# Attention values with the value matrix stationary in column groups, turned back in place

## The chip, the core and the metric

One core of one Trainium2 chip. The metric is the device time of one launch, in microseconds. One launch computes 32 batches of 128 tokens of 512 features. The kernel before takes 2767.58 us, the median of 3 runs (2760.34 to 2768.54).

## What is computed

```python
# attention: 32 heads of 16 features; own keys/values from x, adapter keys/values from ctx
q, k, v = (split_heads(layernorm(x) @ W) for W in (Wq, Wk, Wv));  q, k = rope(q), rope(k)
w = softmax(q @ k.T / 4 + mask)                      # own path
a_k, a_v = split_heads(ctx @ Wk), split_heads(ctx @ Wv)
a_w = tanh(gate) * softmax(q @ a_k.T / 4)            # adapter path, a gate per head
x = x + (w @ v + a_w @ a_v) @ Wo
# experts: 8, the 2 best of each token, rows sorted by expert
x = x + moe(layernorm(x), router_w, w1, w2)
```

## The kernel before

The program has two stages. `attention_phase` goes over the 32 batches and ends with the lists of tokens for each expert; `expert_phase` runs 71 tiles of tokens through their experts. The change lies in the first.

In the attention stage each engine has its own instruction stream, and its `step(b, c, d, n, m)` is run once for each batch b. One step works on several batches at once: the values of batch b; on n = b+1 the projections, rotation, scores and maxima; on d = b-1 the output chain; on c = b-2 the entering into the expert lists; on m = b+2 the first norm. Batches 4 to 29 are a loop of two steps, the others are written out. Between engines stand semaphores: an `Event` is counted up by the producer, and a `wait_ge` in the consumer's stream holds that and everything behind it. The streams are strictly in the order in which they are written, so the order of calls in `step` is the schedule.

On TensorE a step is a loop over 16 units u, a unit being four heads of one of two paths (own and adapter). Each runs `scores_T(b, u)` (transposed scores into a bank `st`), then whatever is hung at that u, then `values(b, u-1)`. ScalarE's loop over u takes the exponent `exps(b, u)` (L528) of `st` into `pr`, an fp32 tile of keys by queries for 4 heads, and does the hung copies and fp16 splits. Hung at TensorE's units before: q after unit 1; k, `ctx_turn` and `out_turn` at 2; `places` (the router's counts, which need `sel` of DVE's `router_top`) at 3; `out_project` at 4; `ak` (keys of ctx, needing ScalarE's `ctx_turned`) at 5; `h_turn` at 7, `router` at 8; `stack(n, g)` and `scores(n, g)` from 8 on, g = 0 to 7, one a unit. `stack` 0 needs DVE's `ak_low`. Behind the loop: v, avp, `x_turn`, `max_turn` (the split maxima are transposed), whose result DVE copies to `mT` (L731). The first `scores_T` of the next step waits for it.

`values` (L1097), for each head: `pr[:, path, j, :]` (128 keys by 128 queries, fp32) is the stationary operand, and the head's 17 columns of `vv` (16 features and a column of ones, whose product is the sum of the exponents) are streamed. The result is 128 queries by 17 columns of a bank `av`; a bank holds 8 heads by 2 paths, and there are two banks, used in turn. Each fp32 matmul is two passes of weight load and matmul in the trace.

DVE copies each full bank to `avs` in SBUF (`values_out`, L737). The next step begins with `norm_out` (L742 reciprocal of the sums, L744 times the gate, L746 adapter half times it), GpSimd's `own_out` (L411, the own half) and `sum_out` (L757) into `nat`. Then the output chain goes on: `out_hi` (ScalarE L538) and `out_low` (DVE L761) split into fp16, `out_turn`, `out_T`, `out_project`, `residual` (L767), norm (GpSimd L416, DVE L781), `h_high`, `h_low` (L786), `ak_low` (L676, of batch n), `h_turn`, `router`.

DVE's `rotate_q` (L685, L689) reads the projected q; GpSimd adds (L376), ScalarE writes `q_high` (L501), GpSimd the rest (L379, `qs`); only then may `rotate_k` write the same `t1`, `t2`, and the same follows for k with `k_high` (L506). ScalarE's `ctx_turned` is L480. GpSimd's `w_slice` (L402, L405) splits the expert weights. GpSimd's `enter_lists` issues 8 indirect DMAs a batch.

## Time and profile before

| what | value |
| --- | --- |
| median of 3 runs | 2767.58 us |
| the profiled execution | 2786.29 us |
| its span, first to last instruction | 2784.5 us |
| mean granted TensorE clock | 0.83 |
| TensorE matmul, busy | 2405.2 us (86%) |
| TensorE weight load, busy | 1746.0 us (63%) |
| VectorE (DVE) | 1409.8 us (51%) |
| ScalarE (ACT) | 1178.9 us (42%) |
| GpSimd (POOL) | 946.0 us (34%) |
| costliest group: values matmuls, L1097 | 636.5 us, 4096 of 292 ns |
| their weight loads | 628.6 us, 4096 of 233 ns |

The profile is of one execution, by the hardware profiler. PE is TensorE's matmuls, PEld its weight loads. Busy time is the union of the instructions of a group; matmuls are pipelined, so the mean duration of one is longer than the distance between two. The clock is given as a share of 2.4 GHz, 0.50 being 1.2 GHz. In the views in order of time, neighbouring instructions of one line stand in one row, and brackets give the idle time before it and the engine that ended it. "Low" and "high" below are the fp16 splits unless the clock is meant.

### The profile page before, as it was taken

What the parts mean: (1) busy time and instruction counts of PE and PEld (TensorE: products, weight loads), DVE (VectorE), ACT (ScalarE), POOL (GpSimd) and SP (SyncE); (2) the same over time, 40 slices, a digit from 0 to 9 for tenths busy, and PEclk for the clock granted to TensorE, in tenths of its full rate; (3) what the DMA queues carried; (4) which work ended last, traced back from release to release, by engine and by line L of the source; (5) the groups of instructions that cost most, each with busy time, mean ns of one, the idle gap of its engine ahead of it and who ended that gap; (6) DMA issues with size and microseconds to landing.
All of it is one profiled execution on the core that took longest, in us unless ns stands there. A gap on an engine that the chain in (4) does not pass through costs nothing. (4 is left out here: it accounts for less than half of the span.)

```text
span 2784.5 us, 55409 instructions
## 1 busy us (share of the span) xinstructions
PE 2405.2 (86%) x18441; PEld 1746.0 (63%) x18442; DVE 1409.8 (51%) x4993; ACT 1178.9 (42%) x2100; POOL 946.0 (34%) x948
## 2 busy tenths in 40 slices
PE   4999898889888979898888888888888836999997
PEld 2777666667666756576666666666666624666664
DVE  4466555556555645555555555555555433333332
ACT  3554444444444434344444444444444304444443
POOL 2223333333333333333333333333333223444443
PEclk7898887788788878787878787888788858999999
DMA  2010000000000000010000000000000204444444
GB/s 88 15 38 28 22 23 23 22 23 22 23 22 23 22 13 27 11 32 17 27 16 27 18 25 21 22 23 22 23 22 19 44 14 106 83 83 83 83 83 68
DMA packets 65264, 98.06 MB, mean 35 GB/s; under 512 B 24512, under 2 KB 28608, under 8 KB 64512
## 3 DMA queue, kind: packets, MB, share of 16 engines
q0 software_dynamic: 24096, 37.51, 7.7%
q1 hardware_dynamic: 40928, 57.30, 6.8%
q8 instruction: 156, 2.56, 0.4%
q14 instruction: 84, 0.69, 0.1%
HBM read 59.12 MB, written 35.65 MB: 34 GB/s over the span
## 5 line engine op out<-in xcount | busy, mean ns | idle before, releaser
L1097 PE MATMUL av<-vv,pr 128*128 128x17 f32 x4096 | 636.5, 292 | 6.2 <-ACT pr L528 6.2
L1097 PEld LDWEIGHTS av<-vv,pr 128*128 128x128 f32 x4096 | 628.6, 233 | 20.2 <-ACT pr L528 6.8
L528 ACT ACTIVATE pr<-st 128x512 f32<-128x512 f32 x512 | 305.0, 596 | 587.0 <-PE st L1083 408.6
L707 DVE TENSOR_REDUCE mx<-md 128x4 f32<-128x512 f32 x256 | 176.7, 690 | 340.4 <-remote 214.4
L1051 PE MATMUL md<-kk,qz 128*128 128x128 f16 x2048 | 214.9, 255 | 136.1 <-DVE mx L707 74.7
L1415 PE MATMUL y<-w1s,hgT 128*128 x1704 | 279.2, 314 | 4.4 <-ACT hgT L1329 4.4
L425 POOL DMA_INDIRECT lists<-row,posi x256 | 249.6, 975 | 85.4 <-issue 85.4
L710 DVE CUSTOM_DVE_ANT_0 md<-md,msk 128x128 f32<-128x128 f32 x1024 | 265.0, 321 | 0.0
L1051 PEld LDWEIGHTS md<-kk,qz 128*128 128x128 f16 x2048 | 157.4, 115 | 167.8 <-issue 112.3
L411 POOL TENSOR_TENSOR avs<-avs,rc 128x512 f32<-128x512 f32 x32 | 34.6, 1082 | 662.8 <-DVE rc L742 662.8
L1074 PE MATMUL st<-qz,kk 128*128 128x256 f16 x1024 | 213.8, 293 | 27.8 <-issue 20.1
L520 ACT ACTIVATE qz<-ma 64x256 f16<-64x256 f16 x512 | 191.6, 374 | 104.4 <-remote 86.7
L1083 PE MATMUL st<-mT,hsel 96*128 96x128 bf16 x2048 | 225.7, 238 | 1.1 <-issue 1.1
L1415 PEld LDWEIGHTS y<-w1s,hgT 128*128 128x128 f16 x1704 | 164.2, 98 | 95.8 <-issue 4.9
L737 DVE COPY avs<-av 128x272 f32<-128x272 f32 x128 | 56.5, 441 | 313.9 <-PE av L1097 278.0
L1083 PEld LDWEIGHTS st<-mT,hsel 96*128 96x128 bf16 x2048 | 153.3, 107 | 94.9 <-issue 84.7
L1078 PE MATMUL st<-identr,mskp 128*128 128x512 f32 x512 | 209.5, 495 | 0.0
L522 ACT ACTIVATE kk<-ma 128x512 f16<-128x512 f16 x256 | 152.9, 597 | 3.0
L1434 PE MATMUL y<-w2s,yT 128*128 (+1 forms) x639 | 150.3, 379 | 0.9 <-DVE yT L1393 0.9
L982 PE MATMUL ma<-w_v,xT 128*128 128x512 f16 x384 | 146.5, 559 | 0.0
L710 DVE DVE_READ_ACCUMULATOR2_ANT mx<- 128x1 f32 x1024 | 145.0, 142 | 0.0
L1329 ACT ACTIVATE hgT<-px 128x1024 f16<-128x1024 f16 x71 | 72.7, 1024 | 156.7 <-PE px L1405 156.7
(200 smaller groups left out, 3968.7 us busy)
## 6 DMA issues: line engine op xcount, KB each, us to landing
wst<-in_w SPq DMA_DIRECT2D x32, 352.0 KB, 3.3
cin<-in_ctx SPq DMA_DIRECT2D x32, 256.0 KB, 3.5
xin<-in_x SPq DMA_DIRECT2D x32, 256.0 KB, 3.7
out<-x SPq DMA_DIRECT2D x32, 256.0 KB, 2.0
h_pairs<-ohs SPq DMA_DIRECT2D x32, 256.0 KB
lists<-row,posi POOLq DMA_INDIRECT x256
msk<-in_mask SPq DMA_DIRECT2D x32, 64.0 KB, 3.1
lrow<-lists SPq DMA_DIRECT2D x71, 1.0 KB, 3.6
```

The source lines that it names most:

```text
L425: pool.indirect_dma_start(out=dram["lists"], out_offset=bass.IndirectOffsetOnAxis(ap=posi[:, e:e + 1], axis=0), in_=row[:, e, :], in_offse ...
L520: act.activation(qz[r, pairs, j, :], bank[r, 0:2], ACT.Copy)
L522: act.activation(kk[:, :, pairs, :], keys, ACT.Copy).then_inc(stk_o.sem, 1)
L528: act.activation(pr[:, path, :, :], st[path][:, :, :], ACT.Exp).then_inc(p_ex.sem, 1)
L707: dve.tensor_reduce(mx[:, 1, 4 * g:4 * g + 4], sm[1][:, :, :], AX.X, ALU.max).then_inc(s_ad.sem, 1)
L710: i = dve.tensor_tensor_reduce(sm[0][:, j, :], sm[0][:, j, :], msk[:, n.par, :], 1.0, -3.4028235e38, ALU.add, ALU.max, mx[:, 0, h:h + 1])
L1051: i = pe.matmul(sm[path][:, j, :], qz[:, h // 2, h % 2, :], keys[:, h // 2, :], start=True, stop=True)
L1074: pe.matmul(bank[:, 2 * j:2 * j + 2, :], keys[:, p, :], qz[:, p, :, :], start=(j == 0), stop=False, skip_group_check=True)
L1078: pe.matmul(bank[:, :, :], mskp[:, n.par, part, :], identr[:, :].unsqueeze(1).to_broadcast([P, 4, P]), start=False, stop=False, skip_group ...
L1083: i = pe.matmul(bank[:, j, :], hsel[:, h:h + 1].to_broadcast([3 * NH, P]), mT[:, path, :], start=False, stop=(j == 3), skip_group_check=True)
L1097: i = pe.matmul(av[g // 2 % 2][:, h % 8, path, :], pr[:, path, j, :], vv[:, n.par, path, h, :], start=True, stop=True)
L1415: i = pe.matmul(y1[s.par][j][:, 0:F], hgT[:, s.par, a, c, :], w, start=(n == 0), stop=(n == 11))
```

## The change

Four things.

1. `values` takes the 17 columns of `vv` as the stationary operand and streams the 128 queries of `pr`. Head j of a unit writes 17 partitions from partition 32j, so the four heads lie in four column groups of the array. A bank is now [128, 4, 128]: partitions are heads by columns, the rest queries.
2. The result is the wrong way round. ScalarE copies each full bank to `avT` in SBUF (`values_T`), TensorE turns it back by four fp32 transposes into the same bank (`values_back`).
3. DVE normalizes each bank straight from PSUM (`normal`: reciprocal, gate, product, sum into the new tile `on`), four times a batch, three of them among the maxima and one between the split of the maxima and the copy of `mT`. `values_out`, `norm_out`, `sum_out` and GpSimd's `own_out` are gone. The bank is free for new values when its sum is written.
4. The order of the output chain and of what lies around it is another in the streams of ScalarE, DVE and TensorE.

The diff, without declarations of events and the first and last batch:

```diff
--- before.py
+++ after.py
@@ -141,8 +142,10 @@
...
     pr = sb("pr", [P, 2, 4, P], F32)
-    avs = sb("avs", [P, NH, 2, VW], F32)
-    rc = sb("rc", [P, NH, 2], F32)
+    avT = sb("avT", [P, 4, P], F32)
+    rc = sb("rc", [P, 2, 8], F32)
+    part2 = sb("part2", [P, 2, 8, HD], F32)
+    on = sb("on", [P, D], F32)
     nat = sb("nat", [P, D], F32)
...
@@ -169,7 +172,7 @@
     st = [ps(f"st{k}", [P, 4, P], F32) for k in range(2)]
-    av = [ps(f"av{k}", [P, 8, 2, VW], F32) for k in range(2)]
+    av = [ps(f"av{k}", [P, 4, P], F32) for k in range(2)]
     ma = [ps(f"ma{k}", [P, 512], F32) for k in range(2)]
...
@@ -379,8 +383,6 @@
...
         def step(b, c, d, n, m):
-            if d:
-                own_out(d)
             w_slice(b)
...
@@ -405,12 +407,6 @@
...
-        def own_out(n):
-            pool.wait_ge(n_rc.sem, n_rc.at(n))
-            pool.tensor_tensor(avs[:, :, 0, 0:HD], avs[:, :, 0, 0:HD],
-                               rc[:, :, 0:1].to_broadcast([P, NH, HD]), ALU.mult).then_inc(n_o1.sem, 1)
         def norm_h(n):
...
@@ -527,6 +522,12 @@
...
+        def values_T(n, o):
+            act.wait_ge(av_pe.sem, av_pe.at(n, 4 * o + 4))
+            act.wait_ge(v_back.sem, v_back.at(n, o))
+            act.activation(avT[:, :, :], av[o % 2][:, :, :], ACT.Copy).then_inc(v_T.sem, 1)
         def w_slice(n):
...
@@ -535,7 +536,7 @@
...
             act.wait_ge(h2_st.sem(n.shift(-1)), h2_st.at(n.shift(-1)))
-            act.activation(ohs[:, 0, :], nat[:, :], ACT.Copy).then_inc(o_hi.sem, 1)
+            act.activation(ohs[:, 0, :], on[:, :], ACT.Copy).then_inc(o_hi.sem, 1)
...
@@ -561,32 +562,34 @@
...
                 if u == 0:
+                    if d:
+                        out_hi(d)
                     if n:
...
                     w_slice(b)
-                if u == 1 and d:
-                    out_hi(d)
                 if u == 2 and n:
                     q_high(n)
-                if u == 2 and c:
+                if u == 3 and c:
                     router_exp(c)
                 if u == 3 and n:
+                    k_high(n)
                     ctx_turned(n)
-                if u == 3 and d:
+                if u == 4 and d:
                     out_T(d)
-                if u == 4 and n:
-                    k_high(n)
-                if u == 5 and d:
-                    h_high(d)
+                if u >= 5 and u % 4 == 1:
+                    values_T(b, u // 4 - 1)
                 if u == 6 and n:
...
                 if u == 7 and d:
+                    h_high(d)
+                if u == 8 and d:
                     h_transposed(d)
...
                     stack_out(n, u - 8)
+            values_T(b, 3)
             if n:
...
@@ -652,6 +655,8 @@
...
         dve.wait_ge(pool_c.sem, pool_c_all)
+        for bank in av:
+            dve.memset(bank[:, :, :], 0.0)
         dve.tensor_copy(ident16[:, :], identf[:, :]).then_inc(dve_c.sem, 1)
...
@@ -727,38 +732,31 @@
...
             dve.tensor_copy(p3[2], mr[:, :, :]).then_inc(mp3.sem, 1)
+            if b:
+                normal(b, 3)
             dve.wait_ge(mp_t.sem, mp_t.at(n))
...
-        def values_out(n, o):
-            dve.wait_ge(av_pe.sem, av_pe.at(n, 4 * o + 4))
+        def normal(n, o):
+            bank = av[o % 2][:, :, :].rearrange("p (a g) (j c) -> p a (g j) c", a=2, c=VC)
+            dve.wait_ge(v_back.sem, v_back.at(n, o + 1))
+            dve.reciprocal(rc[:, :, :], bank[:, :, :, HD]).then_inc(n_rc.sem, 1)
+            dve.wait_ge(n_rc.sem, n_rc.at(n, o + 1))
+            dve.tensor_tensor(rc[:, 1, :], rc[:, 1, :], tg[:, 8 * o:8 * o + 8], ALU.mult).then_inc(n_rg.sem, 1)
+            dve.wait_ge(n_rg.sem, n_rg.at(n, o + 1))
+            dve.tensor_tensor(part2[:, :, :, :], bank[:, :, :, 0:HD],
+                              rc[:, :, :].unsqueeze(3).to_broadcast([P, 2, 8, HD]), ALU.mult).then_inc(n_o2.sem, 1)
+            dve.wait_ge(n_o2.sem, n_o2.at(n, o + 1))
             if o == 0:
-                dve.wait_ge(n_o.sem, n_o.at(n.shift(-1)))
-            dve.tensor_copy(avs[:, 8 * o:8 * o + 8, :, :], av[o % 2][:, :, :, :]).then_inc(av_s.sem, 1)
-        def norm_out(n):
-            dve.wait_ge(av_s.sem, av_s.at(n))
-            dve.reciprocal(rc[:, :, :], avs[:, :, :, HD]).then_inc(n_rc.sem, 1)
-            dve.wait_ge(n_rc.sem, n_rc.at(n))
-            dve.tensor_tensor(rc[:, :, 1], rc[:, :, 1], tg[:, :], ALU.mult).then_inc(n_rg.sem, 1)
-            dve.wait_ge(n_rg.sem, n_rg.at(n))
-            dve.tensor_tensor(avs[:, :, 1, 0:HD], avs[:, :, 1, 0:HD],
-                              rc[:, :, 1:2].to_broadcast([P, NH, HD]), ALU.mult).then_inc(n_o2.sem, 1)
-        def sum_out(n, x_batch):
-            if x_batch:
-                dve.wait_ge(x_hi.sem, x_hi.at(x_batch))
-                dve.wait_ge(x_lo.sem, x_lo.at(x_batch))
-            dve.wait_ge(n_o1.sem, n_o1.at(n))
-            dve.wait_ge(n_o2.sem, n_o2.at(n))
-            dve.wait_ge(h_hi.sem, h_hi.at(n.shift(-1)))
-            dve.wait_ge(h_lo.sem, h_lo.at(n.shift(-1)))
-            dve.tensor_tensor(heads(nat), avs[:, :, 0, 0:HD], avs[:, :, 1, 0:HD], ALU.add).then_inc(n_o.sem, 1)
+                dve.wait_ge(o_hi.sem, o_hi.at(n.shift(-1)))
+                dve.wait_ge(o_lo.sem, o_lo.at(n.shift(-1)))
+            dve.tensor_tensor(heads(on)[:, 8 * o:8 * o + 8, :], part2[:, 0, :, :], part2[:, 1, :, :],
+                              ALU.add).then_inc(n_o.sem, 1)
...
             dve.wait_ge(o_hi.sem, o_hi.at(n))
-            dve.tensor_tensor(ohs[:, 1, :], nat[:, :], ohs[:, 0, :], ALU.subtract).then_inc(o_lo.sem, 1)
+            dve.tensor_tensor(ohs[:, 1, :], on[:, :], ohs[:, 0, :], ALU.subtract).then_inc(o_lo.sem, 1)
...
@@ -774,10 +772,11 @@
...
-        def norm_h(n):
+        def norm_h(n, x_batch):
             dve.wait_ge(h_rs.sem, h_rs.at(n))
-            dve.wait_ge(o_hi.sem, o_hi.at(n))
-            dve.wait_ge(o_lo.sem, o_lo.at(n))
+            if x_batch:
+                dve.wait_ge(x_hi.sem, x_hi.at(x_batch))
+                dve.wait_ge(x_lo.sem, x_lo.at(x_batch))
             dve.tensor_scalar(nat[:, :], x2[:, :], mv[:, 1, 0:1], mv[:, 1, 3:4], ALU.subtract,
...
@@ -853,31 +852,27 @@
...
         def step(b, c, d, n, m):
-            if d:
-                norm_out(d)
-                sum_out(d, n)
             if n:
                 ctx_lo(n)
-                mask_lo(n)
             if d:
...
             if n:
-                rotate_q(n)
+                mask_lo(n)
             if c:
                 router_top(c)
-                router_counts(c)
             if n:
+                rotate_q(n)
                 rotate_k(n)
             if c:
+                router_counts(c)
                 router_weights(c)
-            values_out(b, 0)
             if d:
                 residual(d)
-                norm_h(d)
+                norm_h(d, n)
                 h_low(d)
...
                 ak_low(n)
-            values_out(b, 1)
+            normal(b, 0)
             if d:
...
@@ -888,15 +883,17 @@
...
                 maxima(n, 1)
-                maxima(n, 2)
-            values_out(b, 2)
+            normal(b, 1)
             if n:
-                for g in range(3, 7):
+                for g in range(2, 5):
                     maxima(n, g)
-            values_out(b, 3)
+            normal(b, 2)
             if n:
-                maxima(n, 7)
-                neg_max(n)
+                for g in range(5, 8):
+                    maxima(n, g)
+                neg_max(n, b)
+            else:
+                normal(b, 3)
...
@@ -1091,12 +1086,19 @@
...
             if u % 4 == 0:
-                pe.wait_ge(av_s.sem, av_s.at(n, u // 4 - 1))
+                pe.wait_ge(n_o.sem, n_o.at(n, u // 4 - 1))
             for j in range(4):
                 h = 4 * g + j
-                i = pe.matmul(av[g // 2 % 2][:, h % 8, path, :], pr[:, path, j, :], vv[:, n.par, path, h, :],
-                              start=True, stop=True)
+                i = pe.matmul(av[u // 4 % 2][VC * j:VC * j + VW, 2 * path + g % 2, :], vv[:, n.par, path, h, :],
+                              pr[:, path, j, :], start=True, stop=True)
             i.then_inc(av_pe.sem, 1)
+        def values_back(n, o):
+            pe.wait_ge(v_T.sem, v_T.at(n, o + 1))
+            for k in range(4):
+                i = pe.transpose(av[o % 2][:, k, :], avT[:, k, :], identf[:, :])
+            i.then_inc(v_back.sem, 1)
...
@@ -1131,21 +1133,24 @@
...
                     k(n)
+                if u == 3 and d:
+                    out_turn(d)
+                if u == 3 and n:
                     ctx_turn(n)
-                if u == 2 and d:
-                    out_turn(d)
-                if u == 3 and c:
+                if u == 4 and c:
                     places(c)
-                if u == 4 and d:
-                    out_project(d)
                 if u == 5 and n:
                     ak(n)
-                if u == 7 and d:
+                if u == 5 and d:
+                    out_project(d)
+                if u >= 6 and u % 4 == 2:
+                    values_back(b, u // 4 - 1)
+                if u == 8 and d:
                     h_turn(d)
-                if u == 8 and d:
-                    router(d)
                 if u >= 8 and n:
                     stack(n, u - 8)
+                if u == 9 and d:
+                    router(d)
                 if u >= 9 and n:
...
@@ -1155,6 +1160,7 @@
...
                 avp(n)
+            values_back(b, 3)
             if m:
...
             if n:
```

## Rows read from the trace of the kernel before

**Rows 1.** Line 731: count, duration in ns, first and last start.
```profile
L731 DVE COPY mT<-md x32: 286/287/290, 70.9 to 2193.1; 96x256 bf16<-96x256 bf16 x32
```

**Rows 2.** Slices: length, busy time by engine, granted clock, DMA share, GB/s.
```profile
1941.00:1943.00 2.00, 2.00 (x12) 1.23 (x11) 0.00 (x0) 0.00 (x0) 1.40 (x1) 0.88 0.00 0
...
1965.00:1967.00 2.00, 1.67 (x11) 1.67 (x11) 0.28 (x3) 0.35 (x1) 1.69 (x2) 0.60 0.03 1
...
1985.00:1987.00 2.00, 2.00 (x9) 0.85 (x8) 0.00 (x0) 0.53 (x1) 0.00 (x0) 0.78 0.00 0
```

**Rows 3.** TensorE in order of time, first half: start, duration, line, names, count.
```profile
1921.58 0.39 PE L1074 MATMUL st<-qz,kk 128*128 128x256 f16 x2 [0.38 <-DVE mT L731]
...
1934.91 0.19 PE L1124 MATMUL md<-sel,tri 128*128 128x8 bf16 x1 [2.68 <-DVE sel L818]
...
1938.41 4.28 PE L982 MATMUL md<-w_o,oT 128*128 128x512 f16 x12
...
1943.78 2.75 PE L982 MATMUL ma<-w_k,cT 128*128 128x512 f16 x12
1946.37 0.96 PE L1097 MATMUL av<-vv,pr 128*128 128x17 f32 x8
...
1951.93 0.27 PE L1027 MATMUL ma<-ident,qs 128*128 128x128 f16 x2
```

**Rows 4.** TensorE in order of time, second half of that batch.
```profile
1952.26 1.02 PE L1097 MATMUL av<-vv,pr 128*128 128x17 f32 x8
1953.13 0.38 PE L1074 MATMUL st<-qz,kk 128*128 128x256 f16 x2
...
1965.73 1.84 PE L1097 MATMUL av<-vv,pr 128*128 128x17 f32 x8
1967.40 0.59 PE L1074 MATMUL st<-qz,kk 128*128 128x256 f16 x2
...
1981.54 4.90 PE L982 MATMUL ma<-w_v,xT 128*128 128x512 f16 x12
```

**Rows 5.** DVE in order of time, same batch, first half.
```profile
1921.23 0.29 DVE L731 COPY mT<-md 96x256 bf16<-96x256 bf16 x1 [5.05 <-PE md L1058]
...
1928.12 0.68 DVE L685 TENSOR_TENSOR t<-ma,rope 128x512 f32<-128x512 f32 x1
...
1931.60 0.23 DVE L802 TENSOR_SCALAR key<-lg,top 128x8 f32<-128x8 f32 x1
...
1932.07 2.12 DVE L808 SCALAR_TENSOR_TENSOR key<-oh,key 128x8 f32<-128x8 f32 x1
...
1935.47 0.69 DVE L685 TENSOR_TENSOR t<-ma,rope 128x512 f32<-128x512 f32 x1
...
1943.88 0.68 DVE L767 SCALAR_TENSOR_TENSOR x<-md,xres 128x512 f32<-128x512 f32 x1
...
1948.35 0.69 DVE L786 TENSOR_TENSOR ohs<-nat,ohs 128x512 f16<-128x512 f32 x1 [0.70 <-ACT ohs L549]
1949.84 1.29 DVE L676 SCALAR_TENSOR_TENSOR aks<-ma,aks 128x512 f16<-128x512 f32 x2 [0.80 <-ACT aks L486]
```

**Rows 6.** GpSimd in order of time, same batch.
```profile
1922.06 1.08 POOL L411 TENSOR_TENSOR avs<-avs,rc 128x512 f32<-128x512 f32 x1 [19.50 <-DVE rc L742]
...
1932.04 2.13 POOL L379 TENSOR_TENSOR qs<-t,qs 128x1024 f16<-128x1024 f32 x1 [1.17 <-ACT qs L501]
```

**Rows 7.** ScalarE in order of time, same batch.
```profile
1932.76 1.02 ACT L480 ACTIVATE cT<-ma 128x1024 f16<-128x1024 f16 x1
...
1939.15 1.05 ACT L506 ACTIVATE ks<-t 128x1024 f16<-128x1024 f32 x1
```

**Rows 8.** Groups of ScalarE and DVE by line: busy us, mean ns.
```profile
L528 ACT ACTIVATE pr<-st 128x512 f32<-128x512 f32 x512 | 305.0, 596 | 587.0 <-PE st L1083 408.6 <-remote 171.5 <-PE av L1097 5.8
...
L689 DVE TENSOR_TENSOR t<-ma,rope 128x256 f32<-128x256 f32 x128 | 47.5, 411 | 0.0
...
L742 DVE RECIPROCAL rc<-avs 128x64 f32<-128x64 f32 x32 | 17.5, 546 | 33.0 <-issue 32.9
```

More of the change, by code:

```diff
@@ L39 @@
 VW = HD + 1
+VC = 32
 LB = 4
@@ L202, in attention_phase @@
     m_part, mp3, mp_t, m_T = ev("m_part", 4), ev("mp3"), ev("mp_t"), ev("m_T")
-    t_pe, p_ex, av_pe, av_s = ev("t_pe", 2 * GROUPS), ev("p_ex", 2 * GROUPS), ev("av_pe", 2 * GROUPS), ev("av_s", 4)
-    n_rc, n_rg, n_o1, n_o2, n_o = (ev(n) for n in ("n_rc", "n_rg", "n_o1", "n_o2", "n_o"))
+    t_pe, p_ex, av_pe, n_o = ev("t_pe", 2 * GROUPS), ev("p_ex", 2 * GROUPS), ev("av_pe", 2 * GROUPS), ev("n_o", 4)
+    v_T, v_back = ev("v_T", 4), ev("v_back", 4)
+    n_rc, n_rg, n_o2 = (ev(n, 4) for n in ("n_rc", "n_rg", "n_o2"))
     o_hi, o_lo, o_tp, o_T, o_p, x_2 = (ev(n) for n in ("o_hi", "o_lo", "o_tp", "o_T", "o_p", "x_2"))
@@ L439, in last @@
             pool.iota(iot, pattern=[[1, SLOTS]], base=0, channel_multiplier=0).then_inc(iot_d.sem, 1)
-            own_out(n)
             norm_h(n)
@@ L712, in maxima, with neg_max @@
             i.then_inc(s_own.sem, 1)
-        def neg_max(n):
+        def neg_max(n, b=None):
             dve.wait_ge(s_own.sem, s_own.at(n))
@@ L912, in last @@
         def last(n):
-            norm_out(n)
-            sum_out(n, None)
             router_top(n.shift(-1))
@@ L919, in last @@
             residual(n)
-            norm_h(n)
+            norm_h(n, None)
             h_low(n)
```

## The prediction

> **What bounds the kernel now.** I read the page first (time shares), then the stretch of the attention loop in one batch, engine by engine, in order of time, and last the granted clock in slices of that batch. The copy of the transposed maxima, line 731, comes once a batch and marks its end: 32 times from 70.9 to 2193.1 us, so 2122.2/31 = 68.46 us a batch [rows 1]. I take the batch from 1921.23 us on [rows 5] as the type and count its times from there ("+6.9"). TensorE carries the batch, with a few short stalls. The reader should see three things. First, the values matmuls (line 1097) are led by their weight loads: a unit of four heads is 8 loads of a 128-column fp32 `pr` and 8 matmuls of 17 columns, and the next work starts 0.87 us after it at full clock (1952.26 to 1953.13) and 1.67 us after it at 1.2 GHz (1965.73 to 1967.40) [rows 4]; 16 units make 14 us at full clock, 20% of a batch. Second, TensorE's stalls cost twice. It waits 2.68 us for the router's choice before `places` [rows 3], and runs at 1.2 GHz behind it: 12 matmuls of `out_project` take 4.28 us where the 12 of `ak` take 2.75 [rows 3]; the clock is back in the slice 1941 to 1943 [rows 2]. A second low stretch runs from the slice 1965 to 1967 (0.60, after stalls of 0.9 and 0.5 us) to the slice 1985 to 1987 (0.78) [rows 2], some 20 us. Third, the output chain (sum, out_turn, out_project, norm, h_turn, router) lies beside TensorE's work: its h parts are ready before `h_turn` wants them.
>
> **The change, part by part** (new durations are estimates from the nearest rows).
>
> *Values with 17 stationary columns, `pr` moving.* No row has an fp32 stream of 128 columns nor an output in a column group. Lower end of one pass: an fp16 matmul of 512 columns every 0.216 us (2.59 us for 12, 1943.78 to 1946.37 [rows 3]), so 0.054 us for 128. Upper end: the 128-column fp32 load, 0.87/8 = 0.109 us, two clocks a column [rows 4]. I take the upper, because it is the same operand in the same type. A head's two passes go to one column group and must follow each other; passes of neighbouring groups may overlap. In order of issue that is 5 steps instead of 8: 0.55 us. Going from whole-array work to column groups and back costs between 0 and two matmul latencies; two matmuls of 128 columns take 0.27 us from first start to last end [rows 3], so one latency is 0.27 - 2 x 0.054 = 0.16 us. I take one: 0.71 us a unit, bounds 0.11 (all four groups at once, cheap pass) and 8 x 0.109 + 0.33 = 1.20. Against 0.87 that saves 0.16 a unit at full clock, 0.3 at 1.2 GHz.
> The Trainium skill (TensorEngine Tiling, Overview and Key Properties) allows a column-tiled matmul of up to 32 columns up to 4 times the speed, and says that a change of tiling mode drains TensorE. The first rule is the second rival below, the second is why the switch has a price; no run here shows either yet.
>
> *Turning back.* 16 fp32 transposes a batch, 4 at a time, each with a 128-column fp32 load: 0.109 each by the load row, 0.44 us for four at full clock, 0.87 at 1.2 GHz; below, half of it (0.22), above, double (a second pass). ScalarE gains 4 copies of 128x512, 0.60 each [rows 8]; it is idle enough in units 5, 9, 13 and behind unit 15.
>
> *Normalization.* DVE loses the four copies, `norm_out` and `sum_out`; the latter two held it from +0.2 to +4.1. GpSimd loses `own_out`, 1.08 us [rows 6]. DVE gains four times: reciprocal of 128x16 (between 0.17 and the 0.55 of 64 columns [rows 8], 0.26), gate product 0.19, product from PSUM 0.41 as line 689's [rows 8], sum 0.28: 1.14 us and some gaps, say 1.25. Three are beside TensorE's work. The fourth stands between the split of the maxima and the copy of `mT`: avp ends, transposes 0.44, then 1.25 us, beside which x_turn, max_turn and their latency (0.9) run. So `mT` comes 0.44 + about 0.6 us later; the next batch's first matmul waits for it, 0.35 us before the matmul even now [rows 3, 5].
>
> *The other order at the front.* ScalarE now does out_hi before ctx_hi, so behind exps 0 (done at about +2.1) and two copies of 0.6 ctx_hi ends at about +3.3. DVE then: ctx_lo and out_low, 0.69 each as h_low of the same shape [rows 5], and a quarter-size mask_lo, to +4.9. Then the router's choice, now ahead of rotate_q. It took 5.4 us (from rotate_q's end to `places` at 1934.91 [rows 3, 5]), of which 1.9 in one 8-column instruction of 2.12 us that lies under GpSimd's qs, 2.13 us from 1932.04 [rows 5, 6], against 0.23 for its like [rows 5], and 1.0 in another. Alone it is 2.6 us; with some GpSimd w_low beside it I take 3.0. So rotate_q starts at +7.9, not +6.9. From there by the rows: rotate_k can start 6.1 us later (qs ends 1934.17, rotate_q started 1928.12 [rows 5, 6]), +14.0; its 1.4 us, GpSimd's sum 1.27, then k_high 1.05 [rows 7]: +17.9. ctx_turned, 1.02, stood before k_high and ran at 1932.76, +11.5 [rows 7]; it now stands **behind** k_high in ScalarE's queue: +18.9. Behind it wait exps 4 and out_T. Who waits for ctx_turned is `ak`, and it now stands before out_project.
> TensorE meanwhile: the 2.68 us wait for `places` is gone (the choice is made by about +7.9), nothing slows units 2 to 4, and it has finished scores_T 5 at about +13.5. It then waits for ctx_turned until +18.9: 5.4 us, twice the wait removed. The clock falls again. In the second low stretch it came back in the slice from 1985, about 4 us into the 512-column projection that began at 1981.54 [rows 2, 4]. With 4.4 us at half rate, 10 matmuls are done and 14 take 3.0 us: ak and out_project end at +26.3 (bounds: 24.1 at full clock, 29.1 without recovery). Before, the unit behind them, values 4, began at +25.1 [rows 3].
> Now the output chain is late: from `residual` to the end of h_low 1948.35 + 0.69 - 1943.88 = 5.2 us, and ak_low behind it 1.25 [rows 5]: stack 0, which needs ak_low, goes at about +32.9 instead of +30.7 [rows 3]. **+2.2 us.** Cheaper values units 0 to 6 bring nothing, as they lie beside these waits.
>
> *From stack 0 to the end* (units 7 to 15): five units at full clock -0.8, four at 1.2 GHz -1.2; turning back at units 10, 14 and the end 0.44 + 0.87 + 0.44 = +1.75; router now behind stack 0, +0.3; fourth normalization +0.6. **+0.65.**
>
> **Sum.** +2.85 us a batch over 30 batches (the first two have no router or output part; the expert stage isn't touched) = +85 us. The profiled execution took 2786.29 us with its surroundings (span 2784.5), 0.7% over the median of 2767.58; the difference is carried over: 2786 + 85 = 2871 profiled, 2853 as a median; forecast 2850 us.
>
> **Rivals.**
> *Clock returns earlier (faster).* Place: the low stretch of about 20 us at units 13 to 15. There values are short streams behind long loads and the clock stays low for three units; in the new form the array streams 128 columns nearly all the time. The engine rose behind dense 512-column work both times. If it rises at values 14, at +56, 8.5 us of half-rate work become 4.3: 4.3 us a batch, 2850 - 129 = 2721. It decides once more than 5.7 us of that work goes to full clock. Against it: `pr` moves into 17 of 128 columns only, and the stalls at scores 4 and 5 stay.
> The Trainium skill (TensorE: Matmul & The Clock Gate, "What's actually happening") says that recent activity of the array releases the clock; it would favour this rival.
> *Four groups at once.* A unit costs 0.22 to 0.35 us. Units 7 to 15 save another 0.45 and 0.9 each, 5.9 us, of which DVE's maxima (about 1.7 us a unit against TensorE's 2.2) leave about 5: 2850 - 150 = 2700. For it speaks that the four outputs have their own partitions; against it the two passes a head. This is the 4 times of the page named above.
> *No overlap, full price for switching.* Unit 1.20: +0.5 x 5 + 0.9 x 4 = +6 us, 2850 + 183 = 3030.
> *The front hides.* If the choice takes its 2.6 us, rotate_q comes no later and out_project regains the clock at once, only the +0.65 and about 0.3 stay: about 2790; a little luck in the units and it is no change.
>
> **Chances.** Forecast 0.48, own range 2790 to 2920 (bounds of ak and out_project -2.2 to +2.8 us, of turning back -0.9 to +1.8, taken part way together). Clock earlier 0.22; four groups 0.12; no overlap 0.10; front hides 0.08. A measurement of this kernel can tell about 0.3%, 8 us, from no change. Faster: 0.34 and a sliver, 0.35; within 0.3%: 0.08; slower: 0.57. The range for 8 in 10 has to reach into both faster rivals and part of the dear one: 2690 to 2960.
>
> **What would show it.** Right: TensorE idle for about 5 us before `ak`, released by ScalarE's ctx_turned, no wait before `places`, low clock at ak; stack 0 at +33; `mT`'s copy behind DVE's sum; 71.3 us a batch. Wrong: values units with a pitch under 0.4 or over 1.0 us; transposes over 0.2 us each; second low stretch under 14 us; ctx_turned before +16. What would upset it most is the pitch of a values unit, the one number that no row shows.

## The result, and the profile after

The kernel after takes 2895.24 us (median of 4 runs, 2885.08 to 2900.36), the kernel before 2768.06 us in the same comparison (4 runs, 2760.34 to 2778.68). The ratio is 1.0444, 95% interval 1.0412 to 1.0476: 4.4% slower. The forecast was 2850 us, 3.0% slower, inside a range of 2690 to 2960. Sign and range were right. The experiments show that two of its terms were far off in opposite directions, so that the sum came close partly by luck.

What answers to the groups shown of before is in section 5 of the page of after: line, engine, operation, count, then busy us and mean ns, then idle time before it and what ended it.

```profile
L1092 PE MATMUL av<-pr,vv 128*17 128x128 f32 x4096 | 227.4, 300 | 59.5 <-ACT pr L523 56.8
L1092 PEld LDWEIGHTS av<-pr,vv 128*17 128x17 f32 x4096 | 72.6, 98 | 154.0 <-ACT pr L523 65.9
L977 PE MATMUL ma<-w_k,cT 128*128 128x512 f16 x384 | 157.6, 595 | 174.6 <-ACT cT L475 169.3
L712 DVE TENSOR_REDUCE mx<-md 128x4 f32<-128x512 f32 x256 | 176.4, 689 | 380.4 <-remote 253.2
```

The values matmuls, the costliest group of before with 636.5 us, take 227.4, and their loads 72.6 instead of 628.6. That is 409 us less of matmuls in a kernel that became 127 us longer. The next two rows say where to look. The 512-column matmuls of `ak` wait 169.3 us in all for `ctx_turned` (31 times, 5.5 us each), which they did not do before. And DVE's maxima wait 253.2 us for "remote", a release for which the trace names no engine.

The attention loop, from the first to the last copy to `mT`, in the view of windows (length, busy us and count of PE, PEld, DVE, ACT, POOL, granted clock, DMA share, GB/s), first the kernel before, then after:

```profile
70.90:2193.10 2122.20, 1870.07 (x14581) 1402.91 (x14580) 1189.50 (x4175) 939.17 (x1730) 676.47 (x597) 0.81 0.07 22
```

```profile
72.10:2316.00 2243.90, 1656.94 (x15077) 975.22 (x15076) 1149.96 (x4427) 998.83 (x1854) 635.58 (x568) 0.84 0.07 21
```

Over 31 batches that is 68.5 and 72.4 us a batch. The loop grew by 121.7 us, more than the span (2893.1 against 2784.5 us): all that was lost was lost here. TensorE was busy for 88% of it and now is for 74%. It isn't the bound any more: the batch is set by chains of waits.

One batch in order of time; it begins with `mT`'s copy at 1285.2, from which the offsets below count. TensorE:

```profile
1289.61 0.41 PE L1092 MATMUL av<-pr,vv 128*17 128x128 f32 x8
1289.95 0.39 PE L1069 MATMUL st<-qz,kk 128*128 128x256 f16 x2
...
1296.92 0.17 PE L1126 MATMUL md<-sel,tri 128*128 128x8 bf16 x1
...
1304.59 5.30 PE L977 MATMUL ma<-w_k,cT 128*128 128x512 f16 x12 [5.61 <-ACT cT L475]
1309.68 2.99 PE L977 MATMUL md<-w_o,oT 128*128 128x512 f16 x12
1312.60 0.41 PE L1092 MATMUL av<-pr,vv 128*17 128x128 f32 x8
...
1313.87 0.61 PE L1100 MATMUL av<-identf,avT 128*128 128x128 f32 x4
1314.41 0.41 PE L1092 MATMUL av<-pr,vv 128*17 128x128 f32 x8
...
1319.38 0.27 PE L1022 MATMUL ma<-ident,qs 128*128 128x128 f16 x2 [0.67 <-DVE aks L681]
...
1323.18 0.63 PE L1092 MATMUL av<-pr,vv 128*17 128x128 f32 x8
1323.75 0.61 PE L1069 MATMUL st<-qz,kk 128*128 128x256 f16 x2
...
1342.83 0.58 PE L1046 MATMUL md<-kk,qz 128*128 128x128 f16 x4 [2.72 <-DVE mx L712]
```

ScalarE, whose queue holds `ctx_turned` (L475) behind `k_high` (L501):

```profile
1302.56 1.06 ACT L501 ACTIVATE ks<-t 128x1024 f16<-128x1024 f32 x1 [4.51 <-POOL t L380]
1303.53 1.01 ACT L475 ACTIVATE cT<-ma 128x1024 f16<-128x1024 f16 x1
...
1336.99 0.60 ACT L523 ACTIVATE pr<-st 128x512 f32<-128x512 f32 x1 [3.85 <-remote]
```

DVE, and below it GpSimd, in the second half of the batch:

```profile
1342.00 0.69 DVE L712 TENSOR_REDUCE mx<-md 128x4 f32<-128x512 f32 x1 [7.07 <-remote]
```

```profile
1331.34 1.06 POOL L421 DMA_INDIRECT lists<-row,posi  x1 [0.17 <-issue]
...
1340.30 0.96 POOL L421 DMA_INDIRECT lists<-row,posi  x1 [0.30 <-issue]
```

The reader should see four things. A unit of values is over after 0.34 us (1289.61 to 1289.95), where it took 0.87 [rows 4]. `ak` starts 5.61 us late and its 12 matmuls run at half clock: 5.1 us until the next line, where they took 2.6 [rows 3]. Around +50 three engines, TensorE, ScalarE and DVE, stop within a few us of each other, and DVE goes on at 1342.00, 0.7 us after GpSimd has issued the last of its eight indirect DMAs (the writes to the expert lists; 1340.30 + 0.96), with TensorE behind it. And the clock is low in three short stretches of this batch, each shown here by one of its slices:

```profile
1301.00:1303.00 2.00, 0.00 (x0) 0.00 (x0) 1.58 (x7) 0.44 (x1) 1.26 (x1) 0.50 0.00 0
...
1321.00:1323.00 2.00, 1.70 (x26) 1.62 (x24) 0.95 (x5) 1.98 (x6) 0.00 (x0) 0.50 0.88 249
1327.00:1329.00 2.00, 2.00 (x34) 1.63 (x31) 1.27 (x6) 1.74 (x4) 0.00 (x0) 0.95 0.00 0
1341.00:1343.00 2.00, 0.17 (x3) 0.20 (x4) 1.00 (x4) 0.13 (x1) 1.64 (x2) 0.50 0.01 1
```

The first, from the wait for `ctx_turned` through `ak`, lasts 10.2 us (1299.9 to 1310.1), the second and the third 6.8 us each: 23.8 us in all. In the batch of before the second lasted some 20 us [rows 2]. So that stretch is shorter, but over all batches the low time hardly fell: 23 us a batch against 26 (table below).

### The profile page after: what moved, and what is told of

It is laid out like the page before. It is cut to its first block and busy times, and to the rows that moved or that the text cites. A ratio compares the mean times of both kernels' runs of the same rounds, so it can differ in the third digit from the quotient of the medians.

```text
span 2893.1 us, 56875 instructions
## 1 busy us (share of the span) xinstructions
PE 2180.5 (75%) x18953; PEld 1299.7 (45%) x18954; DVE 1367.2 (47%) x5251; ACT 1240.0 (43%) x2228; POOL 902.1 (31%) x916
## 5 line engine op out<-in xcount | busy, mean ns | idle before, releaser
L1046 PE MATMUL md<-kk,qz 128*128 128x128 f16 x2048 | 222.0, 252 | 196.4 <-DVE mx L712 110.4
L712 DVE TENSOR_REDUCE mx<-md 128x4 f32<-128x512 f32 x256 | 176.4, 689 | 380.4 <-remote 253.2
L977 PE MATMUL ma<-w_k,cT 128*128 128x512 f16 x384 | 157.6, 595 | 174.6 <-ACT cT L475 169.3
L1092 PE MATMUL av<-pr,vv 128*17 128x128 f32 x4096 | 227.4, 300 | 59.5 <-ACT pr L523 56.8
L407 POOL TENSOR_TENSOR w1s<-wst,w1s 128x704 f32 (+1 forms) x32 | 52.3, 1633 | 696.6 <-ACT w1s L533 696.6
L1046 PEld LDWEIGHTS md<-kk,qz 128*128 128x128 f16 x2048 | 150.3, 112 | 253.9 <-issue 137.8
L1073 PE MATMUL st<-identr,mskp 128*128 128x512 f32 x512 | 194.5, 463 | 0.0
L977 PEld LDWEIGHTS ma<-w_k,cT 128*128 128x128 f16 x384 | 50.7, 139 | 264.4 <-ACT cT L475 174.6
L1092 PEld LDWEIGHTS av<-pr,vv 128*17 128x17 f32 x4096 | 72.6, 98 | 154.0 <-ACT pr L523 65.9
```

The source lines that it names most:

```text
L977: i = pe.matmul(bank[:, 0:cols], xt[:, a, c, :], w[:, c, z, :], start=(n == 0), stop=(n == 11))
L1046: i = pe.matmul(sm[path][:, j, :], qz[:, h // 2, h % 2, :], keys[:, h // 2, :], start=True, stop=True)
L1073: pe.matmul(bank[:, :, :], mskp[:, n.par, part, :], identr[:, :].unsqueeze(1).to_broadcast([P, 4, P]), start=False, stop=False, skip_group ...
L1092: i = pe.matmul(av[u // 4 % 2][VC * j:VC * j + VW, 2 * path + g % 2, :], vv[:, n.par, path, h, :], pr[:, path, j, :], start=True, stop=True)
```

## The experiments

Each is a change to the kernel after (or before, where said). Ratios are to the kernel before, timed beside it. Line numbers in rows are those of the kernel that ran. The runs were made on several chips, and the kernel before, timed each time beside them, took from 2754 to 2788 us. So two experiments of different numbers are best compared by their ratios, and a difference of less than about 1 us a batch between their times can't be told from that of the chips.

**1. New values, old order.** The calls in the streams of ScalarE, DVE and TensorE stand where they stood before; `values_T` and `values_back` stay.

```diff
                 if u == 3 and n:
+                    ctx_turned(n)
+                if u == 3 and d:
+                    out_T(d)
+                if u == 4 and n:
                     k_high(n)
-                    ctx_turned(n)
-                if u == 4 and d:
-                    out_T(d)
+                if u == 5 and d:
+                    h_high(d)
...
             if n:
-                mask_lo(n)
+                rotate_q(n)
             if c:
                 router_top(c)
+                router_counts(c)
             if n:
-                rotate_q(n)
                 rotate_k(n)
```

> The changed kernel with the order of the output chain and of what lies around it put back as before in all streams; values, turning back and normalization stay as changed. Theory A (the order is the cost: ScalarE's ctx_turned behind k_high holds TensorE 5.6 us a batch at half the clock behind it): the wait before ak is gone, the wait of 2.7 us before places is back, and with a values unit of 0.34 us instead of 0.87 the kernel is faster than before, 2700 to 2750 us. Rival B (turning back, ScalarE's copies and DVE's four normalizations are the cost): it stays at 2850 to 2900 us.

Measured: 2634.22 us, ratio 0.9594 (0.9535 to 0.9654), 4.1% faster than before and below the range that was given.

**2. New order alone,** put into the kernel before: the same calls moved, but for `out_hi`, which stays at unit 1; old `values` and old normalization.

> The kernel before with only the new order in ScalarE's units 2 to 8, DVE's first part and TensorE's units 2 to 9; values, copies and sums as before. Theory A: a wait of about 5 us before ak released by ctx_turned, 3 to 5 us a batch, 2860 to 2920 us. Rival B: the order costs little by itself, 2760 to 2790 us.

Measured: 2996.53 us, ratio 1.0857 (1.0788 to 1.0925). The sign was expected, the size was not: 8.6% against at most 5.5%. TensorE in one of its batches:

```profile
1276.71 1.01 PE L975 MATMUL ma<-ident,xcs 128*128 128x128 f16 x8 [2.52 <-DVE t L688]
...
1286.26 4.16 PE L981 MATMUL ma<-w_k,cT 128*128 128x512 f16 x12 [2.56 <-ACT cT L480]
```

Two waits stand in the front of the batch, one for `rotate_q`, which now comes behind the choice, and one for `ctx_turned`.

With these two the four combinations of order and values are measured, up to the place of `out_hi`: 1, 0.959 (values), 1.086 (order), 1.044 (both). The two effects add up, -4.1% and +8.6% to +4.5%.

**3. `ctx_turned` ahead of `k_high`** on ScalarE, all else as after:

```diff
                 if u == 3 and n:
+                    ctx_turned(n)
+                if u == 4 and n:
                     k_high(n)
-                    ctx_turned(n)
```

> The changed kernel with one thing moved: ScalarE's k_high goes from unit 3, ahead of ctx_turned, back to unit 4. Theory A: ak waits no longer than for exps 3 (under 1 us), the clock stays up there, 4 to 6 us a batch less: 2720 to 2780 us. If the wait only passes to the next thing in the chain (exps 4 and out_T now stand behind k_high, so out_project waits instead of ak), less than 2 us a batch: 2840 to 2880 us.

Measured: 2737.2 us, ratio 0.9932 (0.9906 to 0.9957). One call moved makes the slower kernel one that is 0.7% faster than before: 72.4 us a batch become 67.4. `ak` doesn't wait for ScalarE then, but it still waits, for the bank that `rotate_k` reads, and still runs at half clock:

```profile
1221.74 5.28 PE L978 MATMUL ma<-w_k,cT 128*128 128x512 f16 x12 [2.30 <-DVE t L695]
```

**4. Number 3, and DVE's old order:** the router's choice behind `rotate_q`, its counts and `mask_lo` in their old places.

> The kernel of e3 with DVE's order at the front also as before (rotate_q ahead of the router's choice, router_counts ahead of rotate_k). It stands between e3 (2737 us) and e1 (2634 us); what is left to e1 is then TensorE's order and the later units of out_T, h_high, h_transposed. If rotate_q's delay is the main part of the rest: 2650 to 2690 us. If the output chain's later units are: 2715 to 2745 us.

Measured: 2609.58 us, ratio 0.9454 (0.9423 to 0.9486): 63.4 us a batch, 0.4 less than with the whole old order, and faster than both ranges that were given. So of the order's 8.6 us a batch (72.4 against 63.8), the swap on ScalarE is worth 5.0 and the order on DVE 4.0. What is still in the new order here, TensorE's units and ScalarE's for the output chain, costs nothing that can be told.

**5. The fourth normalization behind the copy of `mT`.**

> The changed kernel with the fourth normalization of a batch moved from ahead of the copy of mT to behind it. The prediction put its price at 0.6 us a batch: 18 us less, 2870 to 2885 us. Rival (DVE's normalization is hidden beside x_turn and max_turn, or its delay only passes to out_hi): no change within 8 us.

Measured: 2844.48 us, ratio 1.0327 (1.0283 to 1.0371), 0.0117 under that of after. That is 32 us, 1.0 a batch, where the prediction had 0.6. (The times alone differ by 51 us, but the kernel before was 11 us faster beside this run as well.)

**6. The row of eight DMAs earlier** in GpSimd's stream, ahead of `x_low`.

> The changed kernel with GpSimd's enter_lists (8 indirect DMAs, 10 us) moved ahead of x_low, so that it begins some 7 us earlier in the batch. Theory L (while GpSimd issues its indirect DMAs the other engines get stuck, and the stalls of DVE before the maxima are theirs): the idle time of DVE before the maxima of group 4 moves to an earlier group or vanishes behind other waits; the time changes by some 1 to 3 us a batch either way. Rival (the stall belongs to the place in the instruction streams, as fetching of instructions would): DVE still stands about 7 us before the maxima of group 4, and the time stays within 10 us of 2895.

Measured: 2874.99 us, ratio 1.0462 (1.0415 to 1.051), no difference to after that can be told, so the 1 to 3 us a batch were not met. But DVE's stall moved with the DMAs: in a typical batch they were issued from +38.9 to +48.8 and DVE stood still from +45.2 to +50.4.

**7. The eight DMAs twice,** the second eight into a scratch tensor that nobody reads.

```diff
-            for e in range(NE):
+            for e, to in [(e, to) for to in ("lists", "lists2") for e in range(NE)]:
                 pool.indirect_dma_start(
-                    out=dram["lists"],
+                    out=dram[to],
```

> The changed kernel with GpSimd's 8 indirect DMAs of a batch issued a second time, into a scratch tensor that nobody reads: 16 issues, 20 us. Theory L (DVE is stuck until GpSimd has issued its last indirect DMA): the idle time of DVE among the maxima grows from about 7 to about 17 us and ends with the 16th issue; 6 to 10 us a batch more, 3080 to 3200 us. Rival (the stall belongs to the instruction stream or to the data dependences): it stays at about 7 us, and the time under 2950 us.

Measured: 3229.4 us, ratio 1.1705 (1.1661 to 1.175): 334 us more, 10.4 for each of 32 batches and more than was expected, for 8 x 1.26 = 10.1 us more of issuing. GpSimd's own stream isn't the bound, as it still waits 671 us in all (21.6 a batch) for ScalarE before its next work on the expert weights. TensorE in one batch, and GpSimd's last issue beside it:

```profile
1695.24 0.61 PE L1046 MATMUL md<-kk,qz 128*128 128x128 f16 x4 [0.34 <-issue]
1695.78 0.40 PE L1092 MATMUL av<-pr,vv 128*17 128x128 f32 x1
1697.01 0.37 PE L1092 MATMUL av<-pr,vv 128*17 128x128 f32 x1 [0.83 <-issue]
1697.73 0.38 PE L1092 MATMUL av<-pr,vv 128*17 128x128 f32 x1 [0.35 <-issue]
1699.84 0.37 PE L1092 MATMUL av<-pr,vv 128*17 128x128 f32 x1 [1.73 <-issue]
1700.56 0.39 PE L1092 MATMUL av<-pr,vv 128*17 128x128 f32 x1 [0.35 <-issue]
1702.64 0.37 PE L1092 MATMUL av<-pr,vv 128*17 128x128 f32 x1 [1.69 <-issue]
...
1704.04 0.37 PE L1092 MATMUL av<-pr,vv 128*17 128x128 f32 x1 [0.29 <-issue]
```

```profile
1701.11 0.96 POOL L421 DMA_INDIRECT lists<-row,posi  x1 [0.30 <-issue]
```

The eight matmuls of one unit follow each other with no wait between them in the code, and take 0.34 us elsewhere. Here they come one at a time over 8.6 us, the last three of them after the last issue has ended (1702.07). No semaphore holds the queue there; it looks as if the engine lacked its next instruction, which no run shows. DVE was expected to stand once, for about 17 us until the 16th issue. It stood twice:

```profile
1693.48 0.69 DVE L712 TENSOR_REDUCE mx<-md 128x4 f32<-128x512 f32 x1 [7.82 <-remote]
...
1704.87 0.26 DVE L744 RECIPROCAL rc<-av 128x16 f32<-128x16 f32 x1 [9.68 <-remote]
```

Between the two it worked for 1.7 us while seven issues were still to come, and the second stop ended 2.8 us after the last. So the stops go with the row, but they don't simply last until its end.

**8. The row broken up:** number 4, and the eight DMAs two at a time at four places of GpSimd's stream: ahead of `norm_h` and behind it, ahead of `x_low` and behind it.

```diff
+            if c:
+                enter_lists(c, range(0, 2))
             if d:
                 norm_h(d)
+            if c:
+                enter_lists(c, range(2, 4))
             if n:
                 keep_x(n)
...
+            if c:
+                enter_lists(c, range(4, 6))
+            if m:
                 x_low(m)
             if c:
-                enter_lists(c)
+                enter_lists(c, range(6, 8))
```

> The kernel of e7 with the 8 indirect DMAs of a batch issued two at a time at four places of GpSimd's stream (behind rotating k, behind the second norm's power, ahead of x_low, behind x_low). Theory L1 (DVE and the others get stuck only behind the third or fourth of a row of issues): the stall of 7 us among the maxima is gone, 3 to 6 us a batch less, 2430 to 2520 us. Theory L2 (any issue holds the others for as long as it takes): the cost is spread, 2580 to 2640 us; the pieces that stand ahead of GpSimd's powers and rest of x may add to it.

Measured: 2451.07 us, ratio 0.8781 (0.8746 to 0.8816). The same number of DMAs is issued, and the loop is 5.2 us a batch shorter than in number 4. Its window, the maxima's wait in the view of waits (us in total, times, longest), and `ak`:

```profile
72.10:1877.30 1805.20, 1488.74 (x15076) 902.07 (x15076) 1188.16 (x4428) 1004.20 (x1853) 655.21 (x568) 0.95 0.19 26
...
DVE mx L721 <- remote: 99.7, 23, 8.8
...
1253.46 2.75 PE L986 MATMUL ma<-w_k,cT 128*128 128x512 f16 x12 [0.96 <-DVE t L703]
```

The clock is up from 0.91 to 0.95, "remote" fell from 252.5 us to 99.7, and `ak` runs at full clock. The stops are not all gone: in the longest, of 8.81 us, DVE stood from 792.81 to 801.62, though GpSimd's two issues had ended at 793.85.

**9 and 10. The row broken up in the kernel before, and in the kernel after.**

> The kernel before with nothing but the pieces of e9 (two indirect DMAs at a time). Theory S (the stall behind the row of issues is independent of the change and about 5 us a batch, with a low clock behind it): 2560 to 2620 us. If the dear values units fill the stretch anyway, 2680 to 2750 us.

> The changed kernel with the pieces of e9. Theory M (the change's front stretch stays as slow, while the cheaper values units can now pay behind it): the stall and its clock are gone, 2895 goes to 2680 to 2740 us, which is still 80 us or more over e11. If the cheaper units outweigh the order once the stall is gone, at or below e11.

Measured: before in pieces 2777.68 us, ratio 0.9915 (0.9867 to 0.9963); after in pieces 2596.94 us, ratio 0.9321 (0.9291 to 0.9352). Neither range given for before holds it, and after in pieces came out below its first range, as the second branch had it (at or below before in pieces). The window of before in pieces:

```profile
70.20:2181.90 2111.70, 1894.60 (x14580) 1439.39 (x14580) 1167.75 (x4176) 943.05 (x1730) 689.89 (x597) 0.81 0.14 23
```

The maxima's "remote" fell there too, from 214.4 to 52.6 us, and nearly nothing was gained: TensorE is busy for 90% of the loop and stays at a mean clock of 0.81. So it seems that TensorE with the old values needs the time that GpSimd's row took. After in pieces has a clock of 0.92 and gives 9.4 us a batch, though `ak`'s wait is all there:

```profile
PE ma L985 <- ACT cT L483: 170.2, 31, 5.6
```

**11 and 12. Attempts at a better version.** Number 1 with the fourth normalization late and `out_hi` at unit 0, behind `mask_hi`; and number 8 with the fourth normalization late.

> The kernel of e1 (old order, new values) with the fourth normalization behind the copy of mT, and ScalarE's out_hi at unit 0 behind the mask instead of at unit 1. If both terms are on the path, 1 us a batch under e1: 2600 to 2620 us. Rival (the stretch at the end of a batch and the choice of the router set the pace): 2625 to 2645 us, as e1.

> The kernel of e9 with the fourth normalization behind the copy of mT, as in e6. e6 gave 1.6 us a batch against the changed kernel; the same here would be 50 us under e9. If the earlier rows' gain came from a clock that recovered, less than 20 us.

Measured: 2611.78 us, ratio 0.9479 (0.944 to 0.9518), and 2435.33 us, ratio 0.8734 (0.8698 to 0.877). The last is the shortest of all, 12.7% under before, but its interval overlaps with that of number 8: moving the fourth normalization gives nothing there that can be told.

All together, with two columns worked out from the traces: from the copy of `mT` to the first matmul of stack 0 ("front"), and from there to the next copy ("rear"), medians over batches 4 to 28. The time at low clock a batch is 2 x (1 - mean clock) x length, since the traces show the clock at the levels 0.5 and 1 alone; the mean clock's rounding makes it uncertain by 0.7 us.

| kernel | us a batch | mean clock | low clock, us | front | rear |
| --- | --- | --- | --- | --- | --- |
| before | 68.5 | 0.81 | 26 | 30.7 | 37.7 |
| after | 72.4 | 0.84 | 23 | 34.4 | 39.3 |
| 1, old order | 63.8 | 0.90 | 13 | 29.6 | 34.8 |
| 2, order alone | 75.6 | 0.79 | 32 | 35.2 | 42.2 |
| 3, `ctx_turned` first | 67.4 | 0.87 | 18 | 30.8 | 37.5 |
| 4, and choice late | 63.4 | 0.91 | 11 | 26.3 | 37.4 |
| 8, and DMAs in pieces | 58.2 | 0.95 | 6 | 25.6 | 32.6 |
| 9, before in pieces | 68.1 | 0.81 | 26 | 30.9 | 37.6 |
| 10, after in pieces | 63.0 | 0.92 | 10 | 33.5 | 29.8 |

## Why the prediction was right in sign, and where it was wrong

Much of the sum was met in the batch that it described.

- **The wait for `ctx_turned`:** 5.4 us predicted, 5.61 measured; it ended at +18.9 by the sum, +19.4 in the trace (1304.59 less 1285.2). `places` waits for nothing, as predicted. The clock fell in the wait, as predicted, but all of `ak` ran at half clock: 4.4 us at half rate were taken, and it stayed for 5.1. Still values 4 started at +27.4 against +26.3, with the bound 29.1.
- **Stack 0:** +32.9 predicted, +34.2 in this batch, 34.4 as the median. The front grew by 3.7 us where 2.2 were forecast.
- **Normalization:** 1.25 us predicted, 1.23 measured (1319.15 to the end of the sum at 1320.38). **Turning back:** four transposes 0.44 predicted, 0.54 measured (1313.87 to 1314.41). The four start 0.11 us apart, as the load row had it, with one load and one matmul each; the 0.1 us over lies between them and the next unit.
- **Sum:** +2.85 us a batch predicted, +3.9 measured (121.7/31).

**The term of a values unit** failed: 0.71 us were taken, of bounds 0.11 to 1.20; it is 0.34 at full clock, and 0.57 at 1.2 GHz (1323.18 to 1323.75). The raw order of the matmuls shows why. Those of the four heads start within 0.02 us, and the second passes of all four start 0.12 us after the first ones. So one pass of 128 fp32 columns takes about two clocks a column, as the upper bound had it, but the passes of a head don't follow each other before the next head's: all four groups go together, twice. What is left for two switches between the shapes is about 0.34 - 0.24 = 0.1 us, where 0.16 were taken. That is the rival "four groups at once", which had 0.12.

The Trainium skill (TensorEngine Tiling, Overview) allows up to four times the speed where a dimension is at most 32; the rows give 0.87/0.34 = 2.6 times at full clock and 1.67/0.57 = 2.9 at 1.2 GHz. It also says that a change of tiling mode drains TensorE (Key Properties); that price is within those 0.1 us.

**The clock's term** failed too. The rival "clock returns earlier" put 8.5 us of half-rate work in question and had 0.22. The 20 us of the second low stretch are 6.8, and number 1 is at low clock for 13 us a batch where before is for 26. After itself is at 23, as its longer waits bring the low clock back elsewhere. In the old order the new values therefore gain 4.7 us a batch (68.5 to 63.8), where the prediction had them lose 0.65, with nothing gained in front. Both faster rivals were right in mechanism, and yet the kernel became slower.

**The order's term** was right in kind and far too small. Priced were 2.2 us, as the later start of stack 0. It costs 7.2 us in the old kernel (75.6 against 68.5) and 8.6 in the new one (72.4 against 63.8). By the medians of the table it is 4.8 in front and 4.5 behind stack 0. Three steps failed. First, the new front was priced against the old one, but new values in the old order shorten that to 29.6 us, and the new order takes this 1.1 us away. Second, the wait at `ak` was charged as a delay with the half-rate time right behind it. It costs more: taking 3.1 us a batch of it away (169.3 us in all to 72.1) gave 5.0 us a batch. Third, the rear was charged with nothing of the order, and it grows by 4.5 us with either form of values (37.7 to 42.2, 34.8 to 39.3). This part needs GpSimd's row of DMAs: with the row broken up the order costs 4.8 us a batch (63.0 against 58.2), the front carries all of it (33.5 against 25.6), and the rear is even shorter (29.8 against 32.6). (In number 8 only ScalarE's `k_high` and DVE's calls are in the old order, the part that costs by number 4.)

**The fourth normalization** was taken as 0.6 us behind overlap and is worth about 1.0 in after (number 5). **What was not on the list at all** is GpSimd's row of indirect DMAs. It was issued before too, under the same "remote" waits of DVE's maxima (214.4 us in the waits of before), and the prediction read DVE's maxima against TensorE's units without asking why DVE stood still. While TensorE was busy for 88% of the loop, that cost almost nothing (number 9: 0.8%). Once TensorE is light it is a bound: it is worth 5.2 us a batch from number 4 to number 8, and 9.4 from after to number 10. With the row broken up in both, the very change studied here, order and all, makes the kernel faster: 0.9321/0.9915 = 0.940.

The sign was thus forecast for a reason that was half right, the new order at the front. That the sum of +2.85 came near the measured +3.9 is luck: +2.2 and +0.65 stood for some +8.6 and -4.7, two errors that nearly cancel.

**What stays open.** Why issuing indirect DMAs holds the other engines is not shown; that it does is (numbers 6, 7, 8), and that it takes a few of them in a row: in the batch above DVE worked on until 3.6 us behind the start of the first issue. Nor is every stop of this kind beside an issue. Of the 253 us that DVE's maxima wait for "remote" in after, about 163 lie within the rows. Another 70 us are 14 waits that touch no issue at all (before has 9, of 53 us). In the longest no compute engine works from 1125 to 1132, GpSimd included, no DMA packet is under way, and DVE goes on at 1132.86 after 9.87 us. Such waits are gone in numbers 9 and 10, and two are left in number 8 of the 10 in number 4, so they go along with the row, but what holds the engines then is open. They come in some batches and not in others, and the batches of the loop in after last from 65.9 to 85.5 us.

## What to carry to other kernels

A step that is moved in an in-order queue has to be priced by what now stands behind it, down to the engine that idles and the clock it loses, and against what the front could be after the rest of the change, not against what it was. Measure the parts of a change apart: here -4.1% and +8.6% hid in one +4.4%, and moving one call back turned the loss into a small gain. Where several engines stand still together and no semaphore is named, look at GpSimd's DMA issues, also some us earlier, and break rows of them up.

## What the runs showed of the hardware

- fp32 matmuls with 17 stationary columns in four column groups run all four at once, in two rounds of 128 columns, 0.34 us for four heads against 0.87 with the 128-column operand stationary.
- With the 17 columns stationary and the 128 moving, TensorE is at low clock for less of a batch than with the roles exchanged, in the same order of calls: 13 us against 26 (number 1 against before), though it was busy for a smaller share of the loop (79% against 88%). With the row of DMAs broken up it is 10 against 26 (numbers 10 and 9). Whether the longer streams, the shorter loads or the shorter work do it, no run separates.
- Eight indirect DMAs issued in a row by GpSimd (1.26 us each) hold DVE, ScalarE and TensorE for most of the row, DVE for 7.07 us in the batch shown; doubled, they add as much to the batch as their issue time (10.4 us for 10.1). Two at a time, with other work between, the batch is 5.2 us shorter (number 4 to number 8) or 9.4 (after to number 10). The Trainium skill (SBUF — State Buffer, SBUF: two separate sides) names a port pair shared by DVE and GpSimd as the place where engines contend, and says that TensorE and ScalarE wait for no one there. TensorE's single matmuls in number 7 wait all the same, so that port alone doesn't explain this hold.
